# Silu as one ScalarE function in a Mamba round with a gated FFN, and two scan states moved from ScalarE to VectorE

## The reference, cut to what matters

```
xv    = silu(causal_conv4(xn @ W_in) + conv_b)          # 512 x 256
ssm   = xv @ W_x                                         # dt_raw, B (16), C (16)
delta = softplus(dt_raw @ W_dt + b_dt)
h     = scan over tokens of h*exp(delta*A) + delta*B*xv  # 256 x 16 states
s     = ((sum over states of h*C) + xv*D) @ W_out
g     = silu( (silu(xn @ wg.T) * (xn @ wu.T)) @ wd.T )   # hidden 384 = 3 tiles of 128
x     = x + s * g
```

## Time and profile before

| | |
|---|---|
| median of 3 runs | 922.9 us (919.95 to 922.91) |
| profiled execution, its own time | 926.2 us |
| its span | 924.4 us |
| rounds of layer 1 in the span | from 428 us on |
| one steady round | 54.66 us |

### The profile page before, as it was taken

The page is one execution under the profiler, slowest core; times in us unless marked ns, Lnnn a source line. Parts: engine busy times, 40 slices in busy tenths (PEclk is TensorE's granted clock), DMA queues, the critical chain, the costliest instruction groups (busy, mean ns, idle before and its releaser), DMA issues. The chain is left out here.

```text
span 924.4 us, 14633 instructions
## 1 busy us (share of the span) xinstructions
PE 699.5 (76%) x3968; PEld 513.9 (56%) x3969; DVE 704.2 (76%) x1262; ACT 470.2 (51%) x874; POOL 521.0 (56%) x318
## 2 busy tenths in 40 slices
PE   1874888888688775014678997989889898998774
PEld 0761545555444443012247776767677777877763
DVE  5975776666555554784157999998899999999995
ACT  0432555555322221333538677595775867678451
POOL 0213661000000002750286999999899999999994
PEclk9766999999999998556879999999999999999999
DMA  8300110000021111110503122041310413223000
GB/s 229 160 0 15 32 34 11 0 0 0 20 74 47 52 51 35 45 37 0 184 0 116 69 74 100 26 149 47 124 48 24 147 46 127 69 61 113 24 12 12
DMA packets 40047, 55.80 MB, mean 60 GB/s; under 512 B 6584, under 2 KB 29632, under 8 KB 40000
## 3 DMA queue, kind: packets, MB, share of 16 engines
q1 hardware_dynamic: 36224, 50.48, 16.7%
q0 software_dynamic: 2048, 4.20, 1.6%
q10 hardware_dynamic: 1728, 0.57, 0.3%
HBM read 45.54 MB, written 9.70 MB: 60 GB/s over the span
## 5 line engine op out<-in xcount | busy, mean ns | idle before, releaser
L1564 DVE TENSOR_TENSOR_SCAN xnT_all<-psum,nfT_all 128x1024 f32<-128x1024 f32 x128 | 285.4, 2270 | 7.5 <-ACT psum L1414 5.1
L1302 PEld LDWEIGHTS psum<-W_out,xnT_all 128*128 128x128 f32 x2048 | 245.0, 197 | 39.4 <-issue 37.5
L1302 PE MATMUL psum<-W_out,xnT_all 128*128 128x128 f32 x2048 | 247.4, 281 | 17.1 <-DVE acc L1580 17.1
L1414 ACT ACTIVATE psum<-delta,A 128x511 f32<-128x511 f32 x256 | 163.2, 678 | 40.4 <-DVE xnT_all L1564 39.6
L1282 POOL TENSOR_TENSOR nfT_all<-nf_all,du 128x1024 f32<-128x1024 f32 x64 | 149.9, 2369 | 7.8 <-DVE xnT_all L1564 7.8
L1282 POOL TENSOR_TENSOR nfT_all<-attn_all,du 128x1024 f32<-128x1024 f32 x64 | 149.4, 2365 | 4.3 <-DVE xnT_all L1564 3.2
L939 POOL COPY pos_w<-pos 128x4 uint32 x8 | 1.8, 224 | 220.3 <-issue 220.3
L1580 DVE SCALAR_TENSOR_TENSOR acc<-psum,Cc,acc 128x128 f32<-128x128 f32 x352 | 96.6, 340 | 7.8 <-PE psum L1302 7.8
L1302 PE MATMUL psum<-vo_all,wgu 128*128 128x512 f32 (+1 forms) x96 | 51.2, 660 | 26.4 <-DVE hff L1600 24.8
L1302 PE MATMUL psum<-vo_all,W_taps 128*128 (+4 forms) x128 | 59.0, 608 | 1.7 <-DVE psum L1547 1.7
L788 PE MATMUL psum<-gu,xT 128*128 x80 | 46.3, 665 | 15.6 <-DVE hm L871 13.5
(11 more groups left out here) (202 smaller groups left out, 1268.4 us busy)
## 6 DMA issues: line engine op xcount, KB each, us to landing
attn_all<-bt_dram SPq DMA_DIRECT2D x32, 512.0 KB, 5.5
nf_all<-bt_dram SPq DMA_DIRECT2D x32, 512.0 KB, 3.6
xs_dram<-zeros SPq DMA_DIRECT2D x4, 640.0 KB, 7.3
xs_t<-xs_dram SPq DMA_DIRECT2D x40, 64.0 KB, 1.8
ys_dram<-yt SPq DMA_DIRECT2D x40, 64.0 KB, 1.6
x_all<-in_x_dram SPq DMA_DIRECT2D x8, 256.0 KB, 5.7
out_dram<-ow SPq DMA_DIRECT2D x8, 256.0 KB, 2.3
gu<-in_gate_dram SPq DMA_DIRECT2D x1, 1024.0 KB, 6.0
```

The lines of the kernel that those rows point to most:

```text
L1302: return nc.tensor.matmul(o, l, r, start=start, stop=stop)
L1414: ins = nc.scalar.activation(dA[:, i % RA, k, 1:L], delta[:, p, h, 1:L], ACT.Exp, scale=A[:, h, 2 * q + k:2 * q + k + 1])
L1564: nc.vector.tensor_tensor_scan(hring[:, i % R, :, :].rearrange("p n l -> p (n l)"), dA[:, i % RA, :, :].rearrange("p n l -> p (n l)"), dbx ...
```

## The change

Three things change in layer 1.

1. The convolution's silu is ACT's own function Silu, out of PSUM straight into `xv`, one activation for each of the two halves, at q=7 behind `decays(b+1, 0)`. `conv_gate` and the tile `tc_` are gone; `xv` gets a second buffer. A setup instruction that halved `convb` is gone.
2. FFN tiles 0 and 1: PE's `ffn_up(0)` now writes both gates, ACT's `ffn_silu` (q=2, behind the Ln) makes both silus, `ffn_up(1)` then writes both ups, and DVE multiplies twice at q=4. Tile 2 keeps the Tanh form and is done at q=5 on DVE. Before, DVE did the tiles at q=3, 4, 5.
3. `ON_ACT` is (5, 9) and no longer (5, 7, 9, 15): states 7 and 15 are read out by DVE's `add_state`. Two of the three `sum_scaled` of a round on POOL go.

The diff, cut to its core:

```diff
-            ON_ACT = (5, 7, 9, 15)
+            ON_ACT = (5, 9)
...
-                            if q == 1 and end:
-                                sum_scaled(b - 1, 2)
                             if q == 3 and end:
-                                sum_scaled(b - 1, 3)
                                 output()
...
                     def ffn_up(k):
+                        xT = xn1T_all[:, ds((b + 1) * L, L)]
+                        if k == 0:
+                            w("rl", KH)
+                            mm(bank[bM[0]], wgu[:, 0:P], xT)
+                            mm(bank[bM[1]], wgu[:, P:2 * P], xT).then_inc(S["ff_ps"], 1)
+                        elif k == 1:
+                            w("fs", 1)
+                            mm(bank[bM[0]], wgu[:, HID:HID + P], xT)
+                            mm(bank[bM[1]], wgu[:, HID + P:HID + 2 * P], xT).then_inc(S["ff_ps"], 1)
+                        else:
+                            w("hf", 2)
...
-                def conv_silu(c, h):
-                    act.wait_ge(S["xv_ps"], at(c, "xv_ps", h + 1))
-                    act.wait_ge(S["xv"], at(c, "xv", h + 1 - KH))
-                    nc.scalar.activation(tc_[:, h, :], bank[bM[h]], ACT.Tanh, bias=convb[:, h:h + 1])\
-                        .then_inc(S["tc"], 1)
-                    act.wait_ge(S["tc"], at(c, "tc", h + 1))
-                    nc.scalar.activation(bank[bM[h]], bank[bM[h]], ACT.Identity, bias=convb[:, h:h + 1])\
-                        .then_inc(S["yh"], 1)
+                def conv_silu(c, p):
+                    act.wait_ge(S["du"], at(c - 2, "du", 1))
+                    act.wait_ge(S["acc_ps"], at(c - 2, "acc_ps", 1))
+                    for h in range(KH):
+                        act.wait_ge(S["xv_ps"], at(c, "xv_ps", h + 1))
+                        nc.scalar.activation(xv[:, p, h, :], bank[bM[h]], ACT.Silu, bias=convb[:, h:h + 1],
+                                             scale=2.0).then_inc(S["xv"], 1)
...
+                    def ffn_silu():
+                        w("ff_ps", 1)
+                        w("dn_ps", 0)
+                        for k in range(2):
+                            ins = nc.scalar.activation(hff[:, k, :], bank[bM[k]], ACT.Silu)
+                        ins.then_inc(S["fs"], 1)
...
-                        if q == 0 and end:
-                            scale_state(b - 1, 1 - p, 3)
-                        if scan and 3 <= q < 6:
-                            scale_state(b, p, q - 3)
+                        if scan and q in (3, 5):
+                            scale_state(b, p, (q - 3) // 2)
...
                         elif q == 2:
-                            ffn_tanh(0)
                             ln_one_plus()
+                            ffn_silu()
                         elif q == 3:
-                            ffn_tanh(1)
                             one_plus()
                             one_minus()
                         elif q == 4:
-                            ffn_tanh(2)
+                            ffn_tanh()
...
-                        elif q == 6 and ahead:
-                            conv_silu(b + 2, 0)
                         elif q == 7:
                             decays(b + 1, 1 - p, 0)
                             if ahead:
-                                conv_silu(b + 2, 1)
+                                conv_silu(b + 2, p)
...
-                    def conv_gate():
...
                     def ffn_hidden(k):
+                        if k < 2:
+                            w("fs", 1)
+                            w("ff_ps", 2)
+                            nc.vector.tensor_tensor(hff[:, k, :], hff[:, k, :], bank[bM[k]], ALU.mult)\
+                                .then_inc(S["hf"], 1)
+                            return
...
-                        if prep and 3 <= q < 6:
-                            ffn_hidden(q - 3)
+                        if prep and q == 4:
+                            ffn_hidden(0)
+                            ffn_hidden(1)
+                        if prep and q == 5:
+                            ffn_hidden(2)
                         if q == 0:
-                            if prep:
-                                conv_gate()
```

More of the change, by code:

```diff
@@ L1001, in _ @@
                 ins.then_inc(s_diag, 1)
-                nc.vector.tensor_scalar(convb[:, :], convb[:, :], 0.5, None, ALU.mult)
                 for h in range(KH):
@@ L1108, in attention_moe_mamba_ffn @@
             dA = psum[:, 0:2 * RA, :].rearrange("p (r n) l -> p r n l", n=2)
-            tc_ = sb6("tconv", [P, KH, L])
-            xv = sb6("xv", [P, KH, L])
+            xv = sb6("xv", [P, 2, KH, L])
             tf = sb6("tf", [P, L])
@@ L1133, in attention_moe_mamba_ffn @@
             s_o = sem("p6_out_stored")
-            names = {"xv_ps": KH, "yh": KH, "tc": KH, "xv": KH, "ff_ps": KF, "tf": KF, "fa": KF, "hf": KF,
+            names = {"xv_ps": KH, "xv": KH, "ff_ps": KF, "fs": 1, "tf": 1, "fa": 1, "hf": KF,
                      "ssm_ps": 1, "ssm": 1, "C_ps": 1, "C": 1, "dn_ps": 1, "tg": 1, "G1": 1, "dt_ps": KH, "rl": KH,
@@ L1258, in drives @@
                         pool.wait_ge(S["dbx"], at(b, "dbx", 0))
-                        nc.gpsimd.tensor_tensor(du[:, 1 - p, :, :], delta[:, 1 - p, :, :], xv[:, :, :], ALU.mult)\
+                        nc.gpsimd.tensor_tensor(du[:, 1 - p, :, :], delta[:, 1 - p, :, :], xv[:, 1 - p, :, :], ALU.mult)\
                             .then_inc(S["du"], 1)
@@ L1332, in ffn_up @@
                     def ffn_up(k):
[L1333 to L1337, removed]
+                        xT = xn1T_all[:, ds((b + 1) * L, L)]
[9 more added lines that the diff above has]
+                            w("hf", 2)
+                            mm(bank[bM[0]], wgu[:, 2 * P:3 * P], xT)
+                            mm(bank[bM[1]], wgu[:, HID + 2 * P:HID + 3 * P], xT).then_inc(S["ff_ps"], 1)
                     def ssm():
@@ L1341, in ssm @@
                         for h in range(KH):
-                            ins = mm(bank[bM[0]][0:RX, :], W_x[:, h, :], xv[:, h, :], h == 0, h == KH - 1)
+                            ins = mm(bank[bM[0]][0:RX, :], W_x[:, h, :], xv[:, 1 - p, h, :], h == 0, h == KH - 1)
                         ins.then_inc(S["ssm_ps"], 1)
@@ L1363, in skip @@
                             for h in range(KH):
-                                ins = mm(bank[bM[1]][:, j * P:(j + 1) * P], xv[:, h, j * P:(j + 1) * P],
+                                ins = mm(bank[bM[1]][:, j * P:(j + 1) * P], xv[:, 1 - p, h, j * P:(j + 1) * P],
                                          W_outD[:, h, :], h == 0, h == KH - 1)
@@ L1441, in w, with ffn_tanh @@
                         act.wait_ge(S[n], at(b + 1, n, c))
-                    def ffn_tanh(k):
-                        w("ff_ps", k + 1)
-                        w("fa", k)
+                    def ffn_silu():
[4 more added lines that the diff above has]
+                        ins.then_inc(S["fs"], 1)
+                    def ffn_tanh():
+                        w("ff_ps", KF)
+                        w("fa", 0)
                         nc.scalar.activation(tf[:, :], bank[bM[0]], ACT.Tanh, scale=0.5).then_inc(S["tf"], 1)
@@ L1537, in round_ @@
                             if ahead:
-                                conv_silu(b + 2, 1)
+                                conv_silu(b + 2, p)
                 conv_silu(0, 0)
-                conv_silu(0, 1)
                 rounds(act, round_)
@@ L1583, in add_state @@
                                                            ALU.mult, ALU.add).then_inc(S["acc"], 1)
-                    def conv_gate():
[L1586 to L1591, removed]
-                    def ffn_hidden(k):
-                        w("tf", k + 1)
+                    def ffn_hidden(k):
+                        if k < 2:
[4 more added lines that the diff above has]
+                            return
+                        w("tf", 1)
                         w("hf", k)
@@ L1597, in ffn_hidden @@
                             .then_inc(S["fa"], 1)
-                        w("fa", k + 1)
+                        w("fa", 1)
                         w("dn_ps", 0)
```

## The result

The changed kernel takes 932.5 us (median of 4, 929.5 to 936.7) where the kernel before took 921.7 on the same chip: ratio 1.012, 95% interval 1.007 to 1.018. It is slower by 11 us. The forecast was 925.5 with a range of 916 to 932, that is 2.6 us over the median of 922.9 that it started from; the time lies just outside the range.

The account below looks back on a forecast made before the run. Bound: a PE part and a DVE part, chained. 7 rounds x 1.32 = +9.2, less 5.6, less 3.4, plus 2.1, less 1.4 = +0.9, 923.8 in medians; with 1.7 for the clock, 925.5, range 916 to 932.

Parts of the forecast that it names:

- Two chained parts, PE's and DVE's: Steady round of 54.66 us: a PE-bound part of 27.95 chained to a DVE-bound part of 26.71; POOL follows.
- The DVE part grows by 1.3 us: From project(1) to the next ffn_down: -1.42 for multiplies, +1.03 for state 7, +1.7 stall for decays(4).
- The drain of the Trainium skill: At ACT's table switches: some 1380 ns of drain beside the 1283 ns load; the forecast counted none.
- Rival 5: At ACT's table loads: a drain behind each load, 935 us; chance 0.03.
- Once-only terms: Outside steady rounds: first scanning round -5.6, jump back -3.4, last two rounds +2.1, end -1.4.
- (a): First scanning round: the scans and add_state(1) come earlier, -5.6 us, bounds -7 and 0.
- (b): Loop's jump back: with xv made before the jump PE does not stall, about -3.4 us, bounds -4.4 and 0.
- The clock: PE's clock drop at ffn_down after its longer idle: 1.7 us for one round in the forecast.
- most rounds: Rival at ffn_down: the clock drops in most rounds, 5 x 1.7 in place of 1.7, 932 us; chance 0.12.
- my sum: Whole kernel without the clock: +0.9 against the profiled 926.2, giving 927.1, or 923.8 in medians.

Follow-up runs that it names:

- e3: Kernel before with the convolution's part alone (Silu from PSUM, no conv_gate, xv in two buffers): 912.7 us, ratio 0.990.
- e4: Kernel before with only the states changed (ON_ACT (5, 9), two sum_scaled gone): 940.4 us, ratio 1.021.
- e9: Kernel before with the states' change alone, and PE computing the projection of state 9 twice over: 929.7 us, ratio 1.007.
- e10: Changed kernel with state 9's projection computed twice and Tanh in place of Silu in ffn_silu, one table load less a round: 915.1 us, ratio 0.992.
- e2: Changed kernel, PE computing the projection of state 9 twice over ahead of the wait for ffn_down: 926.4 us, ratio 1.005.
- e5: Kernel before with the FFN's part alone, the convolution's two semaphores made one: 924.9 us, ratio 1.0025.
- e8: Changed kernel, ffn_silu behind decays(4), project(6) and project(7) before ffn_up(1), states 6 and 7 before DVE's multiplies, ON_ACT (5, 7, 9): 920.2 us, ratio 0.998.
- e11: Kernel before with the convolution's part alone, plus ON_ACT (5, 6, 7, 9) in place of (5, 7, 9, 15): 908.7 us, ratio 0.985.
- e1: The changed kernel measured again, no edit: 935.8 us, ratio 1.016.
- e6: Changed kernel with ffn_silu moved from step 2 to step 3 on ACT, behind decays(4): 953.3 us, ratio 1.033.

## Why the prediction was right and wrong

*Two chained parts, PE's and DVE's.* Right, and the rest hangs on it. That `conv_gate`'s 1.2 us would buy nothing in a steady round is shown by e3, a round of 54.7; that `sum_scaled` would buy nothing, by e4 and e9; that state 15 is free, by e4's rounds of 55.8.

*The DVE part grows by 1.3 us.* Right: 28.08 and 28.01 for 26.71, with a stall of 1.68 for 1.7 in the rounds shown, multiplies of 1.18 for 1.20, Silu pairs of 1.09 for 1.1. That Silu needs its own load behind Ln was a choice; the trace shows it, five loads a round. e10 shows that the stall is that load.

*The drain of the Trainium skill* ("ScalarE: Activation LUTs", What ACT_TABLE_LOAD costs). By that rule each of the five switches costs 1.38 us more. No run here shows it: Silu starts 0.02 us behind its load, and the end of the Ln to the start of that load is 0.01 us. Rival 5 is out.

*Once-only terms.* Right in sum, less so one by one. (a) -5.6 was -6.6 in the profile, with luck in it: counted from the end of layer 0, `ffn_down` ahead of the scans came 2.6 us later and not 0.6, but took 2.94 us at the full clock where 5.49 were reckoned; without item 2 (e3) the term was -9.9. (b) -3.4 was -2.8: the kernel before lost 4.1 us at the jump back (a period of 58.88 from one `ffn_down` to the next, for 54.75). The changed kernel's 59.03 holds a drop of the clock, so 1.3 are left, and e2, which has no drop there, shows them: 57.40 for 56.0 to 56.1. What is left goes with DVE's own idle, 2.4 to 3.2 us at the jump. It stands in both kernels and is missing in e3, e5, e8 and e11, of which e5 still has `conv_gate`; those four lose 0.1 us or nothing there. Why some programs have it and others don't stays open.

*The clock, the step that failed.* The term was in the sum and mis-sized: one round, +1.7, with bounds of 0 and 7 rounds; "most rounds", 932, had a chance of 0.12. The runs with PE kept at work show what it is at the median: e1 less e2, 935.8 - 926.4 = 9.4 us, and for the states alone e4 less e9, by the ratios 19.2 - 6.8 = 12.4 us. A drop at `ffn_down` costs 1.6, so 9.4 is between five and six of them, and 12.4 is more than all seven: part of it lies in the last two rounds, which the term left out. The reasoning behind "one round" was that an idle of 2.15 us is somewhat shorter than the 2.40 that did it in four of seven. That was an interpolation between gap lengths from a single execution. The idle was as forecast, 2.19 us; what it costs is not read from its length, since the same 2.19 cost 1.6 us in three rounds and nothing in the other four. That the median execution has more drops than three is concluded from the times and the mean clocks; no profile shows one. With the clock taken out the sum holds: e2's 1.005 is +4.3 us, against +0.9 in my sum, and in its profile layer 1 is 2.4 us longer than before, 1.3 of that again lower clock at the end.

*By parts.* Convolution -9.0, FFN +2.3, states +19.2 make +12.5 us; the whole was measured at +11 and +15. No large effect of the parts on each other shows in the total, though at the jump back they don't simply add.

## What to carry to other kernels

Cut a round where the bound changes hands and price each edit by the part it lies in: the same 1.03 us of DVE work is free in one part and costs 7 x 1.03, plus up to a clock drop each, in the other. When an edit lengthens the wait of TensorE ahead of a chain of matmuls that is itself on the critical path, take the dearest case for the clock as the likely one, or give PE work ahead of the wait that may be done twice without harm: that was worth 9.4 us here for 16 matmuls a round. Before a function with a table of its own goes onto an engine that feeds the bound, count the loads between two deadlines, not the loads in a round: two hidden ones cost nothing in a steady round, the third in a row cost all that the edit saved.

## What the runs showed of the hardware that I had not expected

- An idle of 1.9 to 2.2 us of TensorE ahead of `ffn_down`, once a round of 56 us, brought the clock from 2.4 to 1.2 GHz (0.66 over 5 us) in three of seven scanning rounds of the changed kernel's profiles and in five of seven of e4's; with 1.6 to 1.7 us (e6) or 0.4 us of idle (e2, e10) in its place it never fell there in the profiled scanning rounds. The two profiled executions of the changed kernel were hit in the same three rounds.
- The same program took from 926.6 to 940.1 us in six executions, so a single profiled execution can flatter a kernel by 9 us: e1's profile is its fastest execution. The end of layer 0 alone moved by up to 6 us from one profile to another, so profiles are better compared from there on.
- More work on TensorE, put where it would have idled, made the kernel faster: 926.4 against 935.8 us.
- VectorE idled 2.4 to 3.2 us at a hardware loop's jump back in some of these programs and not at all in others, with 4.1 us lost in the kernel before and none in e3 or e5.
